# Mamba scan loop: one product instruction for both halves, an earlier copy of Y, scans ahead of the next block's product, and semaphore clears by ranges

## The reference, cut to what matters

```python
def _selective_scan(x, dt, Bm, Cm, A, D):
    dA = jnp.exp(dt[..., None] * A)
    dBx = (dt * x)[..., None] * Bm[:, :, None, :]
    def step(h, inputs):
        dA_t, dBx_t, C_t = inputs
        h = dA_t * h + dBx_t
        y = jnp.einsum('bdn,bn->bd', h, C_t)
        return (h, y)
    ...
    return jnp.swapaxes(ys, 0, 1) + x * D[None, None, :]
```

## Time and profile before

| | us |
|---|---|
| median of 3 runs | 3063.39 (3062.54 to 3074.31) |
| the profiled execution | 3050.3, its span 3048.6 |
| first experts | 0 to 318.6 |
| Mamba | 318.6 to 1371 |
| experts, ternary, attention, ternary | 1371 to 3048.6 |

### The profile page before, as it was taken

The page is one execution under the profiler, slowest core; times in us unless marked ns, Lnnn a source line. Parts: engine busy times, 40 slices in busy tenths (PEclk is TensorE's granted clock), DMA queues, the critical chain, the costliest instruction groups (busy, mean ns, idle before and its releaser), DMA issues. The chain is left out here.

```text
span 3048.6 us, 38598 instructions
## 1 busy us (share of the span) xinstructions
PE 2538.4 (83%) x11128; PEld 1660.4 (54%) x11128; DVE 2301.2 (75%) x4133; ACT 1779.8 (58%) x3099; POOL 1383.6 (45%) x1486
## 2 busy tenths in 40 slices
PE   6888387878888889777887689969989889887999
PEld 5766143333344344226766568845655556554887
DVE  6788478999999999988787544477778777774444
ACT  3567465556557656524566445547767667765555
POOL 2365588988888888862464630021111111210000
PEclk9999688999999999997999789979999999997999
DMA  2246222222222222211245200020000000001000
GB/s 68 53 134 123 80 71 67 74 68 71 70 69 75 73 70 76 73 52 61 53 139 108 73 21 1 0 95 1 1 1 1 2 1 1 1 1 39 7 8 14
DMA packets 99805, 152.39 MB, mean 50 GB/s; under 512 B 12940, under 2 KB 50572, under 8 KB 99028
## 3 DMA queue, kind: packets, MB, share of 16 engines
q1 hardware_dynamic: 82052, 98.41, 10.5%
q0 software_dynamic: 17040, 51.07, 7.0%
q10 hardware_dynamic: 512, 0.53, 0.1%
HBM read 131.08 MB, written 18.87 MB: 49 GB/s over the span
## 5 line engine op out<-in xcount | busy, mean ns | idle before, releaser
L1730 POOL TENSOR_TENSOR a_hc<-a_H,a_cb 128x512 f32<-128x512 f32 x512 | 623.8, 1230 | 149.6 <-DVE a_H L1598 141.0
L1390 PE MATMUL a_Y<-a_hc,ident 128*128 128x512 f32 x1024 | 532.4, 633 | 51.3 <-POOL a_hc L1730 47.7
L2196 DVE TENSOR_REDUCE a_mx<-a_W 128x1 f32<-128x512 f32 (+3 forms) x768 | 397.1, 551 | 152.9 <-PE a_W L1985 99.0
L2096 ACT ACTIVATE a_pt<-a_W 128x512 f32<-128x512 f32 (+3 forms) x768 | 353.3, 493 | 221.1 <-PE a_W L1998 218.0
L1516 ACT ACTIVATE a_dA<-a_dt,a_aneg 128x512 f32<-128x512 f32 x512 | 340.4, 715 | 209.3 <-DVE a_H L1598 106.0
L1390 PEld LDWEIGHTS a_Y<-a_hc,ident 128*128 128x128 f32 x1024 | 187.0, 196 | 293.5 <-POOL a_hc L1730 185.0
L1998 PE MATMUL a_W<-a_Q,a_K 128*128 128x512 f32 (+3 forms) x768 | 301.5, 398 | 4.8 <-issue 2.7
L1982 PE MATMUL a_W<-a_K,a_Q 128*128 128x512 f32 (+3 forms) x768 | 272.5, 361 | 21.7 <-DVE a_mx L2196 10.9
L2337 POOL TENSOR_TENSOR a_spare<-a_zero 128x1 f32<-128x1 f32 x128 | 27.8, 217 | 575.5 <-ACT a_pt L2096 575.5
L1324 PE MATMUL a_Bp<-a_bcs,a_sel 128*128 128x512 f32 x256 | 179.4, 702 | 95.6 <-DVE a_H L1598 88.3
L712 POOL DMA_INDIRECT m_xg<-m_xrows,m_gidx x184 | 194.9, 1059 | 120.9 <-DVE m_didx L596 65.4
(11 more groups left out here) (330 smaller groups left out, 6332.7 us busy)
## 6 DMA issues: line engine op xcount, KB each, us to landing
a_cb<-a_crow SPq DMA_DIRECT2D x256, 256.0 KB, 3.1
m_orows<-m_yt SPq DMA_DIRECT2D x46, 256.0 KB
a_Q<-attention_zeros POOLq DMA_DIRECT2D x3, 2048.0 KB, 13.7
t_wst<-ternary_w SPq DMA_DIRECT2D x22, 256.0 KB, 2.7
m_xrows<-m_pool SPq DMA_DIRECT2D x16, 256.0 KB, 2.3
m_xg<-m_xrows,m_gidx POOLq DMA_INDIRECT x184
out<-x SPq DMA_DIRECT2D x8, 256.0 KB, 2.3
m_wg<-moe_ws SPq DMA_DIRECT2D x2, 516.0 KB, 4.5
```

Source lines behind the costliest of these rows:

```text
L1390: pe.matmul(Y[:, h, :], ident[:], hc[:, g % HCRING, :], start=False, stop=v == NS - 1).then_inc(s_y, 1)
L1730: pool.tensor_tensor(hc[:, G % HCRING, :], H[:, s, span], cb[:, v % RING, :], ALU.mult).then_inc(s_hc, 1)
L2096: act.activation(pt[:, u % PR, 0:BLK - r * P], W[:, 3 + u % 3, 0:BLK - r * P], ACT.Exp).then_inc(s_exp, 1)
L2196: dve.tensor_reduce(dst, W[:, s % 3, 0:min(BLK, (t + 1) * P - c * BLK)], AX, ALU.max)\
```

## The change

- `bx` and `Bp` become one PSUM tensor `BX` of five banks. Rows go to banks 0, 4, 1 in turn, first-half products to banks 2 and 3, so that the two outputs of a step always have one regular stride, and one `tensor_tensor` writes both halves, reading the row twice. 512 product instructions become 256 of twice the size.
- On DVE a step is now one product and then the two scans of the step before. In a block's first step both last scans of the block before stand ahead of the product and of its wait for u.
- PE gets one wait more, in the row product for step 2 of each block: the first product of the block must have ended. The new product also waits for the scan of step Q - 2 that last read its first bank, which stands three instructions ahead on DVE itself.
- `drain_y` moves to the head of step 1 on ACT.
- `clear` gives `sem_clear` a range. In the built program 223 clearing instructions become 8.

```diff
     def clear(self):
+        nums = sorted(s.num for s in self.sems)
+        first = [n for n in nums if n - 1 not in nums]
+        last = [n for n in nums if n + 1 not in nums]
...
-                for s in self.sems:
-                    pool.sem_clear(s)
+                for a, b in zip(first, last):
+                    pool.sem_clear(range(a, b + 1))
...
-        bx = ph.ps("bx", [P, 2, BLK])
-        Bp = ph.ps("Bp", [P, BRING, BLK])
+        BX = ph.ps("BX", [P, 2 + BRING, BLK])
...
+                    if Q % NS == 2:
+                        pe.wait_ge(s_bx, 2 * Q - 2)
+                    pe.matmul(BX[:, row_bank(Q), :], sel[:, Q % NS, :], bcs[:, Q // NS % 4, :], start=True, stop=True)\
...
                     for v in range(NS):
+                        if v == 1 and b > 0 and (b - 1) % 4 in (0, 1):
+                            drain_y(b - 1)
...
                             decay(b, v + LEAD)
-                        if v == 1 and b > 0 and (b - 1) % 4 in (0, 1):
-                            drain_y(b - 1)
...
-                            for h in range(HALF):
-                                G = b * UB + 2 * v + h
-                                dve.wait_ge(s_B, b * NS + v + 1)
-                                if G == UB:
-                                    scan(G - 1)
-                                if G % UB == 0:
-                                    dve.wait_ge(s_u, 2 * (b + 1))
-                                dve.tensor_tensor(product(G), u[:, b % 2, h, :], Bp[:, G // 2 % BRING, :],
-                                                  ALU.mult).then_inc(s_bx, 1)
-                                if G not in (0, UB):
-                                    scan(G - 1)
...
+                            Q = b * NS + v
+                            if v == 0 and Q:
+                                scan(2 * Q - 2)
+                                scan(2 * Q - 1)
+                            if v == 0:
+                                dve.wait_ge(s_u, 2 * (b + 1))
+                            dve.wait_ge(s_B, Q + 1)
+                            wait(dve, s_scan, 2 * Q - 3)
+                            dve.tensor_tensor(both_banks(Q), u[:, b % 2, :, :],
+                                              BX[:, row_bank(Q), :].unsqueeze(1).broadcast_to([P, HALF, BLK]),
+                                              ALU.mult).then_inc(s_bx, 2)
+                            if v:
+                                scan(2 * Q - 2)
+                                scan(2 * Q - 1)
```

More of the change, by code:

```diff
@@ L1288, in window, with row_bank, half_bank, both_banks @@
             return g % RING, slice(start, start + BLK), slice(carry, carry + 1)
+        def row_bank(Q):
+            return (0, 4, 1)[Q % BRING]
+        def half_bank(Q):
+            return 2 + Q % 2
+        def both_banks(Q):
+            first, second = half_bank(Q), row_bank(Q)
+            if second > first:
+                return BX[:, first:second + 1:second - first, :]
+            return BX[:, first:(second - 1 if second else None):second - first, :]
         def chunk(c):
@@ L1323, in rows @@
                         pe.wait_ge(s_rest, 2)
-                    pe.matmul(Bp[:, Q % BRING, :], sel[:, Q % NS, :], bcs[:, Q // NS % 4, :], start=True, stop=True)\
+                    if Q % NS == 2:
+                        pe.wait_ge(s_bx, 2 * Q - 2)
+                    pe.matmul(BX[:, row_bank(Q), :], sel[:, Q % NS, :], bcs[:, Q // NS % 4, :], start=True, stop=True)\
                       .then_inc(s_B, 1)
@@ L1580, in product @@
                 def product(G):
-                    return bx[:, G // 2 % 2, :] if G % 2 == 0 else Bp[:, G // 2 % BRING, :]
+                    return BX[:, row_bank(G // 2) if G % 2 else half_bank(G // 2), :]
                 def scan(G):
@@ L1613, in _ @@
                         if has_scan(b):
-                            for h in range(HALF):
-                                G = b * UB + 2 * v + h
-                                dve.wait_ge(s_B, b * NS + v + 1)
-                                if G == UB:
-                                    scan(G - 1)
-                                if G % UB == 0:
-                                    dve.wait_ge(s_u, 2 * (b + 1))
-                                dve.tensor_tensor(product(G), u[:, b % 2, h, :], Bp[:, G // 2 % BRING, :],
-                                                  ALU.mult).then_inc(s_bx, 1)
-                                if G not in (0, UB):
-                                    scan(G - 1)
-                            if G == NB * UB - 1:
-                                scan(G)
+                            Q = b * NS + v
[12 more added lines that the diff above has]
+                                scan(2 * Q - 1)
+                            if Q == NB * NS - 1:
+                                scan(2 * Q)
+                                scan(2 * Q + 1)
                         if (b, v) in RETURNS:
```

## The result

The changed kernel took 3035.88 us in the median (3029.33 to 3039.38, 4 runs), the kernel before in the same comparison 3062.97 (3060.84 to 3074.31, 4 runs). The ratio is 0.989, its 95% interval 0.9868 to 0.9913. The prediction was 3032, with a range of 3017 to 3047, and "faster by over 0.5%".

A forecast was written before the change was run, and what follows sets the result against it. In the Mamba part DVE was taken as nearly the bound, with POOL and PE close behind. Clears 13, product 10, copy 15, less 6.5 for lost lead and additions, gave 31.5 us: 3032 us, range 3017 to 3047.

The forecast's parts named there:

- Clears: At the ends of the six parts: 223 clears become 8, 215 saved at 0.06 us each, 13 us gained.
- Copy of Y: ACT's copy comes earlier, removing PE's stall before step 4 in blocks 2, 6, 10, 14: 15 us gained, 4 to 17.
- Merged product: On DVE in Mamba: one product for two saves 0.04 to 0.05 us a step, 10 us counted.
- The step that counted 12 of 16 steps: In most blocks a wait swallows what the product gains ahead of step 4, leaving 10 us of 11 to 13.
- Last scans: At block starts on DVE: 1.19 us of scan moves into the wait for u, but step 4's row is later; nothing added.
- Lead of PE: PE's rows in Mamba: lead shrinks from 5.1 to 3.4 us, too little at step 4; loss of 4, together 6.5.
- Additions to x in blocks 0 to 5: DVE's additions now precede a scan that POOL used to work on meanwhile, and POOL has no slack: loss of 2.5 us.
- The first (0.14 a step): Merged product on DVE: the whole fixed cost goes, 36 us, 17 more than forecast, 3015 us; chance 0.07.
- The second (slow opening): PE opens Y at the slow rate after all, so the copy gives 4 us, not 15: 3043 us; chance 0.15.
- The third (the lead lost in full, 18): PE's lead costs 1.13 us in every block and again at convolutions, -18 instead of -6.5: 3044 us; chance 0.10.
- The fourth: A range of clears costs as its numbers do and the product has no overlap: 3066 us, no change; chance 0.04.
- The fifth: Slower: bursts lengthen PE's gaps and TensorE's clock falls; granted clock 0.80 would give about 3093 us; chance 0.04.

The follow-up runs named there:

- second comparison: The unaltered changed kernel timed once more beside the kernel before, on another set's chip: ratio 0.9898, median 32.1 us below before.
- single_clears: Changed kernel with one clearing instruction for each semaphore again: ratio 0.9944 to the kernel before, median 18.8 us below it, Mamba part 1030.5 us.
- early_copy_alone: Kernel before with only the copy of Y moved to the head of step 1: ratio 0.995 to before, Mamba part 1032.0 us.
- old_order: Kernel before with the copy of Y at the head of step 1 and clears by ranges: ratio 0.99 to before, Mamba part 1034.6 us.
- two_products: Changed kernel with two products of 512 in place of one of 1024, new order kept: ratio 0.9944 to before, Mamba part 1044.7 us.
- between: Changed kernel with each merged product between the two scans of the step before, except at block starts: ratio 0.9884 to before, Mamba part 1020.2 us.
- last_scan_alone: Kernel before with only the last scan of every block moved ahead of the next block's product and waits: ratio 0.9983, Mamba part 1042.9 us.
- late_copy: Changed kernel with the copy of Y behind the step's decays again: ratio 0.9968 to the kernel before, Mamba part 1053.4 us.
- first group: Four altered kernels (clears, copy of Y twice, products) run on one chip beside the kernel before, whose median there was 2988.12 us.

## Why the prediction was right

The total was right (3032 against 3035.88, and -31.5 against -32.1 in the second comparison), and the Mamba part with its meeting was foretold at 1031 and came at 1030.7. The largest two terms, clears and copy, were right in mechanism and size. Two others were mis-sized, the merged product by 4.4 us and the loss of lead by 4 to 6, and these cancelled. That the total came so close is in this part luck.

| term | predicted, us | measured, us | from |
|---|---|---|---|
| clears | -13 | -13 | meetings; single_clears |
| copy of Y | -15 | -14.6 to -17.2 | early_copy_alone, old_order |
| merged product | -10 | -14.4 | two_products less after |
| lead of PE, with the last scans ahead | a loss of 6.5 (4 and 2.5), and 0 | a loss of 10.1 to 12.7 | two_products less old_order or early_copy_alone; between |
| last scans ahead, with the late copy | 0 | -6.3, of which 3.9 by the opening of Y | last_scan_alone |

**Clears.** Right: five of the six meetings are at 0.4 us, the last at 0.6. A range costs a little by its length (see the last section) but far less than single clears.

**Copy of Y.** Right in mechanism and size, by the row: the stall gone in all four blocks, the opening fast again. The choice between 4 and 17 turned on whether the slow matmuls follow from the gap. Mostly they do: all four openings behind the gap of 3.3 us are slow in the kernel before and in late_copy, and none is where the early copy has removed the gap. But in last_scan_alone only two of the four are slow behind the same gap, so the gap makes the slow opening likely and not certain.

**Merged product.** The overlap term, 0.04 to 0.05 us a step, was mis-sized: it is 0.06, since the double product lasts 1.211 and not the 1.224 us of the one row I had, and its successor starts 0.10 before its end. The step that counted 12 of 16 steps was wrong as well: with the copy early, the wait at step 4 no longer swallows much, and 14.4 of 15 us arrive. The Trainium skill's "VectorE: DVE Perf Modes", section "The DRAIN you can't avoid", has the next operation wait until the pipeline is empty, but the same paragraph lets a next operation that is not held start earlier, which the prediction left out. The rows fit that exception and not the rule (1.11 against 1.21). By the rule alone the saving would have been 0.14 a step.

**Last scans.** "I add nothing" is neither confirmed nor refuted as a sum. In blocks 4 and 8 the row of step 4 is indeed the later event, but in block 12 it is not, and the 1.2 us of scan that fill the wait for u are won there. The 6.3 us of last_scan_alone are mostly the pace of the matmuls that open Y, which the term did not speak of.

**Lead of PE.** This is the term that was mis-sized most. Going from the copy alone to the new order with two products costs 10.1 to 12.7 us, with the last scans in it, and taking one scan of lead back (between) gives 10.1. The working block by block had 6.5. If the last scans won something with the early copy too, the loss of lead alone is larger by as much; that stays open. Shown is that lead is what is short: a scan taken back gives 10.1, rows made earlier 8.9, both 14.2, with the waits for rows falling alongside. The step that failed is the working block by block: "with the scan still owed nothing is won or lost" in block 9, and "blocks 5, 9, 13 nothing". I had let the row come 0.6 us earlier, as the old block's last scan does. The timeline of POOL at the end of block 8, before and then changed, shows why it doesn't keep up with the scan:

```profile
948.97 3.71 POOL L1730 TENSOR_TENSOR a_hc<-a_H,a_cb 128x512 f32<-128x512 f32 x3
952.99 1.26 POOL L1730 TENSOR_TENSOR a_hc<-a_H,a_cb 128x512 f32<-128x512 f32 x1 [0.31 <-DVE a_H L1598]
```

```profile
946.88 1.27 POOL L1763 TENSOR_TENSOR a_u<-a_dt,a_xs 128x512 f32<-128x512 f32 x1
948.12 4.93 POOL L1750 TENSOR_TENSOR a_hc<-a_H,a_cb 128x512 f32<-128x512 f32 x4
```

Before, POOL waits 0.31 us for the block's last scan, which starts at 951.70. In the changed kernel that scan starts 2.1 us earlier, at about 949.6, but POOL has just made u and does the block's last four products without a gap. So it ends only 1.2 us earlier (953.05 for 954.25). PE's opening of Y (959.63 for 960.82) and the row of step 4 (962.66 for 963.85) are the same 1.2 us earlier. DVE is ready for that row 2.9 us earlier, at 962.29 for 965.21. The 0.56 us in hand have become a wait of 1.26, where 0.5 was worked out. (The 12.45 us allowed for DVE took plain scans of 1.13; in this block they carry on, at 1.19, so it should have been 12.8.) In block 14, too, the row came 0.9 us later than worked out.

The waits at step 4 in the changed kernel are 5.50, 2.96, 1.28, 1.25, 0.37, 1.26, 0.38 and 1.24 us in blocks 0, 1, 4, 5, 8, 9, 12 and 13, a sum of 14.2. The 15 that were said agree by chance: the 5.5 of block 0 are the 5.2 of the kernel before, which the prediction passed over when it put the large waits in the blocks with t = 2. Another 7.1 us stand at the row of step 2 in blocks 2, 6, 10 and 14 (1.6 before). These blocks have given part of the copy's gain back there. The row of step 4 in block 0 of the kernel before, timeline of DVE:

```profile
390.19 0.70 DVE L1621 TENSOR_TENSOR a_bx<-a_u,a_Bp 128x512 f32<-128x512 f32 x1 [5.22 <-PE a_Bp L1324]
```

**Additions to x in blocks 0 to 5.** Counted at 2.5. The wait for u at block 1 is 10.87 us in the changed kernel:

```profile
450.81 2.36 DVE L1638 TENSOR_TENSOR a_BX<-a_u,a_BX 128x1024 f32<-128x1024 f32 x2 [10.87 <-POOL a_u L1763]
```

It looks twice as long as before (5.51), but in the kernel before DVE's wait at this place was in two pieces, with the last scan of block 0 between them:

```profile
438.47 1.22 DVE L1598 TENSOR_TENSOR_SCAN a_H<-a_dA,a_Bp 128x512 f32<-128x512 f32 x1 [4.93 <-PE a_Bp L1324]
445.20 0.70 DVE L1621 TENSOR_TENSOR a_bx<-a_u,a_Bp 128x512 f32<-128x512 f32 x1 [5.51 <-POOL a_u L1743]
```

Together that is 10.4, and block 0 is only 0.3 us longer than before. What grew are block 1 (+1.8 without the mark that moved) and block 4 (+2.6), with waits for rows at step 4 of 3.0 and 1.3 and, in block 4, 1.7 us of the gate's wait for the last sums. No run here separates the additions from POOL's backlog, so this term stays open.

**The rivals.** The first (0.14 a step) is refuted by the start of the scan at 1.11. The second (slow opening) did not happen. The third (the lead lost in full, 18) lies above what the runs show, 10.1 to 12.7, which is between it and the forecast of 6.5. The fourth is refuted: both parts gave what was worked out. The fifth did not come: the granted clock of the part is 0.93, before 0.92.

## What to carry to other kernels

Look for who copies the accumulator that the next group of matmuls must open, and put that copy at the head of its engine's queue: two moved lines were worth 15 us here. When instructions are merged, price the order that the merging forces as well as the fixed cost it saves: 0.06 us a step won 14 us, and one scan less of lead lost 10 to 13. After a change that wins, look at which wait is now the largest and hand some lead back; here that gave another 14 us.

## What the runs showed of the hardware that was not expected

- One clear of a range of 47 or 48 semaphores takes 0.289 us, of 27 0.180. The two ranges of the ternary part take 0.178 and 0.044, those of attention 0.153 and 0.067. Single clears take 0.06 each. So a range is not free of its length, but by the first two figures a semaphore more in it costs only some 0.005 us.
- The experts parts, the same code in every kernel here, took 280 to 296 us in the first group and 303 to 324 elsewhere. They differ by chip and by execution (315 and 324 us for the first of them in the first comparison), while Mamba's repeat within 0.4 us for the changed code and 2.6 for the old order with the early copy. A gain of 1% in this kernel is read from its part, not from the profiled span.
- After a gap of 3.3 us on PE the four matmuls that open Y ran at the lower clock level for some or all of their time in ten of twelve cases (four each in the kernel before and in late_copy, two of four in last_scan_alone): 5.2 to 6.6 us in place of 3.7. Without the gap, in the same blocks, they took 3.7. So such a gap mostly costs more than its own length.
